# Context chunks loaded a second time with channels on partitions, in a gated cross-attention kernel

## The reference

```python
lat = layer_norm(_layernorm(x), ln_lat_g, ln_lat_b)
ctx = layer_norm(context, ln_ctx_g, ln_ctx_b)     # (x - mu) * rsqrt(var + eps) * g + b, over the 512 channels
q = (lat @ Wq) as 16 heads of 64
k, v = split(ctx @ Wkv)                           # 16 heads of 64 each
k = apply_rope(k, cos, sin)
attn = softmax(clip(q @ k.T / 8, -11, 11))
x = x + tanh(g_xattn) * ((attn @ v) @ Wo + bo)
x = x + tanh(g_ffn) * int8_matmul(_layernorm(x), rhs)
```

## Time and profile before

| | us |
|---|---|
| median of 3 executions (lowest, highest) | 1489.73 (1487.76, 1489.96) |
| the profiled execution's own time | 1489.53 |
| its span, first to last instruction | 1487.7 |
| projections (TensorE's last product of that stage ends) | 472.8 |
| TensorE busy in the span | 1458.5 (98%) |
| VectorE busy | 1246.0 (84%) |
| ScalarE busy | 706.5 (47%) |
| GpSimd busy | 118.7 (8%) |

### The profile page before, as it was taken

How to read it: one execution, slowest core, us unless ns; L and a number is a source line. 1 busy time by engine, 2 the same in 40 slices (tenths; PEclk the granted TensorE clock), 3 DMA queues, 4 the chain that set the end, 5 groups by cost and what they waited for, 6 DMA issues and landing times. The chain is left out here.

```text
span 1487.7 us, 22575 instructions
## 1 busy us (share of the span) xinstructions
PE 1458.5 (98%) x8090; PEld 886.2 (60%) x8090; DVE 1246.0 (84%) x1108; ACT 706.5 (47%) x823; POOL 118.7 (8%) x71
## 2 busy tenths in 40 slices
PE   8999999999999899999999999999999999999997
PEld 7888888888887344444444444444444444444774
DVE  6756666667655999999999999999999999997997
ACT  4432222222223556565655656565656556564332
POOL 0500000000000300000000000000000000001775
PEclk9999999999999999999999999999999999999998
DMA  7783655555667623523532532541551551402652
GB/s 269 249 260 135 205 170 170 186 157 165 193 172 253 165 48 96 129 60 98 133 70 81 135 92 58 135 101 48 135 127 27 130 134 37 121 16 72 171 169 85
DMA packets 144496, 195.60 MB, mean 131 GB/s; under 512 B 36160, under 2 KB 85312, under 8 KB 138304
## 3 DMA queue, kind: packets, MB, share of 16 engines
q1 hardware_dynamic: 141296, 189.71, 45.3%
q10 hardware_dynamic: 3152, 5.25, 0.9%
HBM read 114.83 MB, written 80.08 MB: 131 GB/s over the span
## 5 line engine op out<-in xcount | busy, mean ns | idle before, releaser
L966 ACT ACTIVATE prob<-score_ps 128x1024 f32<-128x1024 f32 x512 | 483.1, 1032 | 187.1 <-PE score_ps L888 184.3
L900 PE MATMUL value_ps<-prob,v_st 128*64 128x512 f32 x2048 | 468.6, 599 | 4.9 <-DVE prob L1050 4.9
L1066 DVE TENSOR_TENSOR prob_sum<-prob_sum,prob 128x2048 f32<-128x2048 f32 x192 | 446.3, 2325 | 13.6 <-DVE prob L1050 0.2
L888 PE MATMUL score_ps<-q_st,k_st 64*128 64x512 f32 x3072 | 396.7, 403 | 7.9 <-ACT prob L966 5.8
L888 PEld LDWEIGHTS score_ps<-q_st,k_st 64*128 64x128 f32 x3072 | 272.8, 186 | 177.5 <-issue 103.1
L1050 DVE TENSOR_SCALAR prob<-prob 128x4096 f32<-128x4096 f32 x128 | 292.7, 2287 | 41.0 <-ACT prob L966 38.8
L900 PEld LDWEIGHTS value_ps<-prob,v_st 128*64 128x64 f32 x2048 | 135.8, 137 | 272.9 <-issue 265.0
L644 DVE TENSOR_TENSOR k_cos<-k_raw,rope 128x1024 f32<-128x1024 f32 x32 | 39.2, 1225 | 100.0 <-ACT k_raw L548 100.0
L553 ACT ACTIVATE v_out<-proj_ps 128x1024 f32<-128x1024 f32 x31 | 31.9, 1028 | 136.7 <-PE proj_ps L230 136.7
L548 ACT ACTIVATE k_raw<-proj_ps 128x1024 f32<-128x1024 f32 x31 | 31.9, 1029 | 105.1 <-PE proj_ps L230 105.1
L1062 DVE TENSOR_TENSOR prob_sum<-prob 128x2048 f32<-128x2048 f32 x32 | 75.8, 2368 | 1.8 <-DVE prob L1050 0.2
(11 more groups left out here) (123 smaller groups left out, 1333.6 us busy)
## 6 DMA issues: line engine op xcount, KB each, us to landing
k_st<-k_scr SPq DMA_DIRECT2D x128, 256.0 KB, 6.5
k_scr<-k_hi SPq DMA_DIRECT2D x64, 256.0 KB, 2.7
v_scr<-v_out SPq DMA_DIRECT2D x32, 512.0 KB, 3.4
k_scr<-k_lo SPq DMA_DIRECT2D x64, 256.0 KB, 4.0
q_st<-q_scr SPq DMA_DIRECT2D x16, 1024.0 KB, 10.9
v_st<-v_scr SPq DMA_DIRECT2D x16, 1024.0 KB, 13.8
q_scr<-q_hi SPq DMA_DIRECT2D x32, 256.0 KB, 4.3
q_scr<-q_lo SPq DMA_DIRECT2D x32, 256.0 KB, 4.4
```

Source lines behind the costliest of these rows:

```text
L888: last = pe.matmul(score_ps[:, u % BANKS, a, :], k_st[slot][rows, k_part, s * P:(s + 1) * P], q_st[slot][rows, q_part, cols], start=(t == ...
L900: last = pe.matmul(value_ps[rows, :], v_st[slot][:, s, rows], prob[:, b % 2, i, a * CH:(a + 1) * CH], start=(s == 0), stop=(s == STEPS - 1))
L966: act.activation(prob[:, b % 2, u % BATCH_UNITS, :], score_ps[:, u % BANKS, :, :], ACT.Exp, scale=SCALE).then_inc(exped, 1)
L1066: dve.tensor_tensor(total, total, halves[j], ALU.add).then_inc(added, 1)
```

## The change

A second copy of the context is given to the kernel, with the 512 channels of each chunk as rows: `context_t` is (8 x 512, 512). For each context chunk:

- the token-major copy is still loaded, now in rows of four tokens per partition and into slot 0 of `raw` only (`load_rows`), and measured as before (`measure_rows`); root and reciprocal follow (`sqrt_rows`, `invert_rows`), so that `stat` holds mean and 1/deviation;
- SyncE stores `stat` to DRAM in runs of 16 bytes (4 KB in all), waits for that store, and loads both as rows of 512 tokens broadcast over all partitions, 256 KB each (`spread_stats`), into `rows`, which lies in `tok`;
- the channel-major copy is loaded into `ctok`, which lies in `w_stage` (`load_columns`, 1024 KB), and VectorE subtracts the row of means and multiplies by the row of reciprocals, two operations over 128 x 2048 elements (`normalise_columns`); ScalarE applies gain and bias in place (`affine_columns`), and `tok_split` reads `ctok`;
- the 16 transposes of TensorE are gone for the eight context chunks. The four latent chunks are as before.

The places in the streams: `normalise_columns` after the K part of j = 1 on VectorE, `tok_split` after that of j = 2 (it was j = 1), `affine_columns` after `k_raw` of j = 2 on ScalarE, `spread_stats` after the V store of j = 0 on SyncE, the two loads at j = 2. For context chunk 0 they lie in the latent chunks 2 and 3, with n the chunk and m the block of q. The diff, cut to its core:

```diff
@@ sync: new helpers @@
+        def load_rows(c, tok0):
+            if isinstance(c, int) and c == 0:
+                sp.wait_ge(turned, KT * (QCH - 1))
+            else:
+                sp.wait_ge(ctx_moments_made, c)
+            sp.dma_start(raw[:, 0, :, :], context[bass.ds(tok0, CH), :].rearrange("(p t) d -> p t d", t=CT)
+                         ).then_inc(raw_in[0], 16)
+
+        def load_columns(c, slot, tok0):
+            if isinstance(c, int) and c < 2:
+                sp.wait_ge(wkv_lo_made, KT)
+            else:
+                sp.wait_ge(tok_lo_made, QCH + c - 1)
+            sp.dma_start(ctok[slot], context_t[bass.ds(tok0, DIM), :].rearrange("(k p) c -> p k c", p=P)
+                         ).then_inc(ctok_in[slot], 16)
+
+        def spread_stats(c, slot, row):
+            sp.wait_ge(ctx_rstd_made, c + 1)
+            sp.dma_start(stat_scr[bass.ds(row, 2), :].rearrange("f (p t) -> p f t", t=CT), stat[:, slot, :, :]).then_inc(stat_stored, 16)
+            sp.wait_ge(stat_stored, 16 * (c + 1))
+            if isinstance(c, int) and c == 0:
+                sp.wait_ge(tok_lo_made, QCH)
+            for f in range(2):
+                sp.dma_start(rows[:, slot, f, :], stat_scr[bass.ds(row + f, 1), :].broadcast_to((P, CH))).then_inc(rows_in[slot], 16)
@@ sync: latent chunks @@
-                if m == 0:
+                if m == 0 and n + 2 < QCH:
                     load_chunk(n + 2, n % 2, chunk_rows(n + 2))
+                if m == 0 and n + 2 >= QCH:
+                    load_rows(n + 2 - QCH, (n + 2 - QCH) * CH)
+                if (n, m) in ((2, 5), (3, 1)):
+                    load_columns(n - 2, n - 2, (n - 2) * CH)
+                if (n, m) == (2, 7):
+                    spread_stats(0, 0, 0)
@@ sync: context_chunk @@
+                if j == 0 and following:
+                    spread_stats(c + 1, 1 - slot, row)
                 if j == 2 and ahead:
-                    load_chunk(c + QCH + 2, slot, context[bass.ds(tok0 + 2 * CH, CH), :])
+                    load_rows(c + 2, tok2)
+                    load_columns(c + 2, slot, tok2)
@@ scalar @@
+        def affine_columns(c, slot):
+            act.wait_ge(scaled, c + 1)
+            for k in range(KT):
+                act.activation(ctok[slot][:, k, :], ctok[slot][:, k, :], ACT.Identity, bias=gains[:, 3, k:k + 1],
+                               scale=gains[:, 2, k:k + 1]).then_inc(affine_made, 1)
+                if m == 3 and n + 1 == QCH:
+                    affine_columns(0, 0)
@@ scalar: context_chunk @@
+                    if j == 2 and ahead:
+                        affine_columns(c + 1, 1 - slot)
-                if j == 1 and ahead:
-                    affine(c + QCH + 1)
@@ vector @@
+        def normalise_columns(c, slot):
+            spread = [rows[:, slot, f:f + 1, :].broadcast_to((P, KT, CH)) for f in range(2)]
+            dve.wait_ge(ctok_in[slot], 16 * (c // 2 + 1))
+            dve.wait_ge(rows_in[slot], 32 * (c // 2 + 1))
+            dve.tensor_tensor(ctok[slot], ctok[slot], spread[0], ALU.subtract).then_inc(centred, 1)
+            dve.wait_ge(centred, c + 1)
+            dve.tensor_tensor(ctok[slot], ctok[slot], spread[1], ALU.mult).then_inc(scaled, 1)
+                if m == 5 and n + 2 == QCH:
+                    measure_rows(0, 0)
+                if m == 6 and n + 2 == QCH:
+                    invert_rows(0, 0)
+                if m == 1 and n + 1 == QCH:
+                    normalise_columns(0, 0)
@@ vector: context_chunk @@
                 if j == 0 and ahead:
-                    normalise(c + QCH + 1, 1 - slot)
+                    invert_rows(c + 1, 1 - slot)
                 if j == 1 and ahead:
-                    tok_split(c + QCH + 1, 1 - slot)
+                    normalise_columns(c + 1, 1 - slot)
+                if j == 2 and ahead:
+                    tok_split(c + QCH + 1, 1 - slot, ctok[1 - slot])
@@ tensor @@
-                if m == (4 if n == 0 else 3):
+                if m == (4 if n == 0 else 3) and n + 1 < QCH:
                     turn(n + 1, 1 - slot)
-                if j == 1 and ahead:
-                    turn(c + QCH + 1, 1 - slot)
```

More of the change, by code:

```diff
@@ L62, in flamingo_kernel @@
     rec_scr = nc.dram_tensor("rec_scr", (ALLPAIRS, 2, 2, CH), F32, kind="Internal").ap()
+    stat_scr = nc.dram_tensor("stat_scr", (2 * CCH, CH), F32, kind="Internal").ap()
     o_scr = nc.dram_tensor("o_scr", (BATCH, INNER, NQ), F32, kind="Internal").ap()
@@ L103, in flamingo_kernel @@
         with ExitStack() as stage:
-            projections(nc, stage, x, context, cos_t, sin_t, affines, wq, wkv, q_scr, k_scr, v_scr,
+            projections(nc, stage, x, context, context_t, stat_scr, cos_t, sin_t, affines, wq, wkv, q_scr, k_scr, v_scr,
                         ident, ident_bf, ones, eps_col, g_xattn, g_ffn, gates, gate_tanh, w_stage, raw, tok, load_pair,
@@ L231, in split_product, with projections @@
     return last
-def projections(nc, ctx, x, context, cos_t, sin_t, affines, wq, wkv, q_scr, k_scr, v_scr,
+def projections(nc, ctx, x, context, context_t, stat_scr, cos_t, sin_t, affines, wq, wkv, q_scr, k_scr, v_scr,
                 ident, ident_bf, ones, eps_col, g_xattn, g_ffn, gates, gate_tanh, w_stage, raw, tok, load_pair,
@@ L267, in projections @@
     rope = sb("rope", [P, 2, 2, CH])
+    stat = sb("stat", [P, 2, 2, CT])
+    rows = tok[:, :, :].rearrange("p (s f) c -> p s f c", s=2)
+    ctok = [w_stage[:, s, :].rearrange("p (k c) -> p k c", c=CH) for s in range(2)]
     proj_ps = ps("proj_ps", [P, 4, CH])
@@ L297, in projections @@
     WARM_LATE = 10
+    ctok_in = [sem(f"ctok_in{i}") for i in range(2)]
+    ctx_moments_made = sem("ctx_moments_made")
+    ctx_aggregated = sem("ctx_aggregated")
+    ctx_std_made = sem("ctx_std_made")
+    ctx_rstd_made = sem("ctx_rstd_made")
+    stat_stored = sem("stat_stored")
+    rows_in = [sem(f"rows_in{i}") for i in range(2)]
+    centred = sem("centred")
+    scaled = sem("scaled")
     turned = sem("turned")
@@ L384, in chunk_rows @@
         def chunk_rows(n):
-            return x[n * CH:(n + 1) * CH, :] if n < QCH else context[(n - QCH) * CH:(n - QCH + 1) * CH, :]
+            return x[n * CH:(n + 1) * CH, :]
         for t in range(0, CT, 2):
@@ L415, in store_k, with context_chunk @@
                              t[:, s, half, :].bitcast(F32)).then_inc(k_stored[s], 16)
-        def context_chunk(c, slot, ahead, order=IN_TURN):
+        def context_chunk(c, slot, ahead, order=IN_TURN, following=True):
+            row, tok2 = sp.snap(2 * c + 2), sp.snap((c + 2) * CH)
             b, s0, tok0 = sp.snap(c // 4), sp.snap((c % 4) * CH), sp.snap(c * CH)
@@ L527, in _ @@
                     sqrt(1)
[L528 removed]
+                if m == 6 and n + 2 < QCH:
                     sqrt(n + 2)
[L530 removed]
+                if m == 6 and n + 2 == QCH:
+                    sqrt_rows(0, 0)
+                if m == (4 if n == 0 else 3) and n + 1 < QCH:
                     affine(n + 1)
+                if m == 3 and n + 1 == QCH:
+                    affine_columns(0, 0)
                 if n < 2 and m in (4, 6):
@@ L592, in normalise, with measure_rows, invert_rows, tok_split @@
             last.then_inc(normed, 1)
-        def tok_split(n, slot):
+        def measure_rows(c, slot):
+            dve.wait_ge(raw_in[0], 16 * (c + QCH // 2))
+            for t in range(CT):
+                last = dve.bn_stats(moments[:, t, :], raw[:, 0, t, :])
+            last.then_inc(ctx_moments_made, 1)
+            if not (isinstance(c, int) and c < 2):
+                dve.wait_ge(stat_stored, 16 * (c - 1))
+            dve.wait_ge(ctx_moments_made, c + 1)
+            dve.memset(spacer[:, :], 0.0)
+            for t in range(CT):
+                last = dve.bn_aggr(stat[:, slot, :, t], moments[:, t, :])
+            last.then_inc(ctx_aggregated, 1)
+        def invert_rows(c, slot):
+            dve.wait_ge(ctx_std_made, c + 1)
+            dve.reciprocal(stat[:, slot, 1, :], std[:, :]).then_inc(ctx_rstd_made, 1)
+        def normalise_columns(c, slot):
[5 more added lines that the diff above has]
+            dve.tensor_tensor(ctok[slot], ctok[slot], spread[1], ALU.mult).then_inc(scaled, 1)
+        def tok_split(n, slot, source):
             slot_read(dve, n)
             for half in range(2):
-                rows = slice(half * KT // 2, (half + 1) * KT // 2)
-                dve.wait_ge(affine_made, KT * n + rows.stop)
-                last = dve.tensor_copy(tok_hi[:, slot, rows, :], tok[:, rows, :])
+                part = slice(half * KT // 2, (half + 1) * KT // 2)
+                dve.wait_ge(affine_made, KT * n + part.stop)
+                last = dve.tensor_copy(tok_hi[:, slot, part, :], source[:, part, :])
             last.then_inc(tok_hi_made, 1)
             dve.wait_ge(tok_hi_made, n + 1)
-            dve.tensor_tensor(tok_lo[:, slot, :, :], tok[:, :, :], tok_hi[:, slot, :, :].bitcast(F32),
```

(1 more changed line is left out.)

26 lines of the change are left out of this document (16 added, 10 removed).

## The result

The changed kernel takes 1479.39 us (median of 6 runs, 1478.46 to 1481.09) against 1489.64 for the kernel before (6 runs, 1487.58 to 1490.25): a ratio of 0.9936, 95% interval 0.9923 to 0.9948. That is 10.2 us faster, inside the range of the prediction, 3.4 us above its number and 0.9 above the narrower range that it gave for its own mechanism. A second set of runs beside each other gave 0.9935 (0.9921 to 0.9948).

A forecast was written before the change was run, and what follows sets the result against it. TensorE's stream was taken to bound the projections: 14.1 us of turns removed less 0.5 us of border stall gives 13.6 off 1489.53, 1475.9, given as 1476.0; range 1474.0 to 1482.0, own mechanism 1474.5 to 1478.5 (76%).

The forecast's parts named there:

- What bounds the kernel: In the context chunks TensorE's stream is the time; work taken out shortens the kernel unless TensorE gets new waits.
- The removed work: Eight context chunks each lose a turn of 16 transposes, 1.76 us of TensorE's stream: 14.1 us saved.
- The context chunks: VectorE's added 2.7 us a chunk, SyncE's issues and 1.5 MB more DMA are covered by slack: cost nothing.
- the margin of 6.4: In context chunks, statistics rows may land as late as 232.3, with VectorE asking at 225.87, before ScalarE delays TensorE.
- Rival 2: Slower: late statistics in seven context chunks make ScalarE hold back V of j = 3; 1496 at 9.5 us late; 4%.
- The border: Context chunk 0, prepared inside latent chunks 2 and 3 where blocks are shorter, stalls TensorE by 0.5 us.
- Landing after 3.3 us: At the border, the statistics' store issued at 90.35 behind 1024 KB of columns lands at 93.65.
- is covered, with 1.6 us to spare: At the border, SyncE's late q stores free the first `k_raw`, copied by 119.5, before TensorE wants it at 121.1.
- Rival 1: Border costs 3 to 7.6 us as statistics' transfers queue behind 2 MB of columns and rows: 1479 to 1483.5; 16%.
- The formula from the Trainium skill: Transfer costs about 2.0 us plus bytes at 436 GB/s; rows near 96, border free, 14.1 us saved.
- Rival 3: Start of attention doesn't move, being set by a pair's first load and not TensorE: 1489.5 us; 4%.

The follow-up runs named there:

- the run with three trips: Changed kernel plus three more waited 4 KB stores between the statistics' store and its broadcasts in context chunks 1 to 7: 1505.44 us.
- Columns apart: Changed kernel with the column loads of chunks 0 and 1 issued before and after the border: border 41.13 us (unedited 41.82 to 42.90), last group 460.12.
- early statistics: Changed kernel with chunk 0's statistics measured, stored and spread earlier, ahead of the columns' load: border 41.71 us, last group at 460.18 against 462.23.
- early statistics with the next loads late: Changed kernel with chunk 0's statistics earlier and context chunk 1's row and column loads put off: border 41.50 us, last group at 460.33.
- the run in order: Changed kernel with chunk 0's statistics earlier, context chunk 1's loads put off and rotary tables loaded in latent chunk 0: 1474.73 us, ratio 0.9909 to the kernel before.
- the two slowest: Longest borders, each one edit to the changed kernel: tables in latent chunk 2 (46.64 us, time 1482.05); statistics through ScalarE's queue (45.17 us, time 1482.81).
- three edits together: Changed kernel with chunk 0's statistics through ScalarE's queue, columns before and after the border, tables in latent chunk 0: 1478.83 us, ratio 0.9930 to before.

## Why the prediction was right, and where it was off

**What bounds the kernel** was right: TensorE's stream was the time of the projections, and what left it left the kernel, less what the border cost.

**The removed work** was right to the size: 1.76 us a turn forecast, 1.78 measured both by taking them away and by putting them back.

**The context chunks** cost nothing, as forecast. VectorE's two operations last 2.29 us each, ScalarE's gains 2.9, the windows from 300 to 345 us show VectorE busy 34.6 of 45 and the DMA at 0.64 and 210 GB/s (forecast a share near 0.7 and 215). In three of the seven chunks VectorE doesn't wait for the rows, in three it waits 0.8 to 1.2 us and in the first 4.10, which leaves 2.3 of the margin of 6.4. Rival 2 was a real mechanism that needed more than that; its price of the waits alone, 20 us at 2.9 a chunk, was too low, since 18.2 us of them in the run with three trips made the stage 27.8 longer.

**The border** was mis-sized: 0.5 us forecast, 4.7 measured (3.7 to 4.8 over five profiled runs). In the profiled executions this is 4.2 of the 4.4 us between 13.6 and 9.2. The term that failed is "Landing after 3.3 us" for the statistics' store: it took 5.3. The number was the median of q stores in a stretch where the engines' share was 0.5 to 0.9, while the changed kernel puts 1 MB of columns ahead of this store and the share there is 1.00; the prediction named the 1 MB and didn't charge it. The broadcasts took 4.6 instead of 3.3 to 3.9. They had little ahead of them (share 0.31) but four q stores and 1 MB of rows right behind them; that these slowed them is likely, and not shown by itself. The second half is the lag that "is covered, with 1.6 us to spare": SyncE's late q stores were followed only to the first `k_raw`. They reach ScalarE sooner, since `q_hi` of block 6 waits for the landing of block 2's store, 6.5 us after its issue behind 2 MB of loads, and of that nothing was in the sum. Rival 1, with 3 to 7.6 us and a chance of 16%, was what happened; the forecast's own range of 1474.5 to 1478.5 was missed by 0.9 us, and the time lies in the stated range because that took rival 1 in. The formula from the Trainium skill, page DMA: Bandwidth & Descriptors, section Anatomy of one DMA, would have been further off, with no cost at the border. The section gives it for the GpSimd path, one transfer at a time, while all these transfers are SyncE's; and it has no term for what is ahead of a transfer.

**Rival 3**, a start of attention that doesn't move, was wrong: it moved by 9.48 of 9.49 us.

What stays open is how much of the border belongs to the late rows and how much to the late q stores. Columns apart leaves 2.3 us of waits, early statistics 3.3, and early statistics with the next loads late 2.9, so the causes overlap: as one wait goes, the next shows. No run separates them fully, and the last microsecond that remains in the run in order has no named cause. But for that run and the two slowest, the edits moved the border by 1 us or less beyond its unedited spread, in one profiled run each.

## What to carry to other kernels

Work taken out of the stream of the busiest engine pays in full where the rest has slack, and the slack should be worked out link by link to the last harmless moment; here the price of a turn and the margin both held to a tenth of a microsecond. At a border, where blocks are shorter and a chain of two transfers is new, don't price a small transfer by its size or by a median of others: look at what is issued in the microseconds ahead of it, and follow every wait for the landing of stores, not only for loads. A dependent store and reload belongs ahead of the bulk loads and into a stretch where the DMA engines are idle, and what can be loaded long before should not be issued there. Measure the spread of such a border in several profiles of the same code before a single edited run is read.

## What the runs showed of the hardware

A store of 4 KB in runs of 16 bytes landed in 2.3 us at a DMA share of 0.34 and in 5.3 and 7.8 us where the engines were full (shares of 1.06 and 1.02 in the first microseconds from its issue). Issued from another queue, with nothing ahead of it there, it still took 6.2.

Waits of TensorE of 2.32 and 2.62 us left the granted clock at 1.00, and so did one of 3.34 us (statistics early, from 109.5 to 112.8, then 1.00 in every window to 118). But one of 2.93 us (three edits together) and one of 2.94 us were followed by the lower clock, so the length of the wait alone doesn't decide, and what does isn't shown here. The one of 2.94 us, at V of j = 3 in the run with three trips, was followed by some 5.3 us at 0.50, in which groups of four matmuls started 1.7 to 1.9 us apart and not 0.91. So short a wait had not been expected to cost as much again as it lasted: the six groups of that V block took 8.4 us and not 5.4. In that run seven waits of 18.2 us in all made the stage, from the first mark on, 27.8 us longer than in the changed kernel.
